# Token stage of an adaLN-attention-FFN kernel: the last VectorE operation of a weight unit stands behind the second normalising, GpSimd's scaling behind the token combination

## What is computed

```python
x = x + attn(einsum('bct,bcd->bdt', x, weights[conditions]))      # 16 heads, 8 kv heads, rope, top 25 of 64 keys by a router
h = x @ W.T + scaling[a] * (x @ A[a].T) @ B[a].T                  # a = adapter of the sequence
x = x + (gelu_tanh(h @ dequant(gate).T) * (h @ dequant(up).T)) @ dequant(down).T
```

## Time and profile before

| | us |
|---|---|
| median of 3 runs | 2812.93 |
| lowest, highest | 2810.95, 2813.51 |
| profiled execution | 2812.71 |
| its span, first to last instruction | 2811.1 |
| TensorE busy | 2669.4 (95%) |
| VectorE busy | 2182.8 (78%) |
| ScalarE busy | 1227.2 (44%) |
| GpSimd busy | 995.2 (35%) |

### The profile page before, as it was taken

The page is one execution under the profiler, slowest core; times in us unless marked ns, Lnnn a source line. Parts: engine busy times, 40 slices in busy tenths (PEclk is TensorE's granted clock), DMA queues, the critical chain, the costliest instruction groups (busy, mean ns, idle before and its releaser), DMA issues.

```text
span 2811.1 us, 54312 instructions
## 1 busy us (share of the span) xinstructions
PE 2669.4 (95%) x19200; PEld 2446.2 (87%) x19200; DVE 2182.8 (78%) x3724; ACT 1227.2 (44%) x2425; POOL 995.2 (35%) x1189
## 2 busy tenths in 40 slices
PE   5888998898899999999999999999999999999998
PEld 4777887787789999999999999999999999999998
DVE  6877777877578888888888888888888888756555
ACT  3445445454344444444444444444444444444443
POOL 4454434434244343434344343434334343300000
PEclk7999999999999999999999999999999999999999
DMA  3223232322676586668667766966776686657552
GB/s 119 74 97 100 78 98 87 102 75 94 237 283 246 215 341 252 256 237 346 228 231 294 309 228 223 358 259 226 268 314 248 233 311 264 235 213 282 190 193 88
DMA packets 197576, 599.87 MB, mean 213 GB/s; under 512 B 21224, under 2 KB 80488, under 8 KB 185200
## 3 DMA queue, kind: packets, MB, share of 16 engines
q1 hardware_dynamic: 162160, 496.89, 48.1%
q0 software_dynamic: 35328, 101.82, 9.7%
HBM read 417.83 MB, written 180.75 MB: 213 GB/s over the span
## 4 chain that ended last, share of the span: by engine, by line
PE 76%; DVE 15%; issue 4%; ACT 2%; DMA 2%; POOL 1%; SPq 0%; DVEq 0%; POOLq 0%; ACTq 0%
PE bank_a L881 22%; PE down L889 21%; PE bank_b L881 12%; PE proj L711 11%; PE bank_c L881 6%; DVE inter L1426 2%; DVE inter L1417 1%; DVE lut_line L1215 1%; PE scores L751 1%; PE scores L760 1%; DVE inter_parts L1433 1%; ACT inter L1128 1%; DVE hs L1242 1%; PE pv L776 1%; DVE probs L1308 1%
## 5 line engine op out<-in xcount | busy, mean ns | idle before, releaser
L881 PEld LDWEIGHTS bank_a<-h_in,gu_slot 128*128 128x128 f32 x6144 | 855.7, 190 | 74.0 <-ACT copy_p L1164 8.7
L881 PE MATMUL bank_a<-h_in,gu_slot 128*128 128x256 f32 x6144 | 899.0, 282 | 6.0 <-ACT copy_p L1164 5.8
L889 PE MATMUL down<-d_slot,inter_parts 128*128 128x512 f32 x3072 | 835.8, 394 | 2.0 <-DVE inter_parts L1433 2.0
L889 PEld LDWEIGHTS down<-d_slot,inter_parts 128*128 128x128 f32 x3072 | 527.6, 190 | 68.8 <-DVE inter_parts L1433 2.4
L881 PE MATMUL bank_b<-h_in,gu_slot 128*128 128x256 f32 x3072 | 456.3, 284 | 17.5 <-DVE up_val L1439 17.5
L592 POOL TENSOR_TENSOR lut_v<-lut_v,signed_scale 128x512 f32<-128x512 f32 x96 | 123.7, 1289 | 871.3 <-DVE lut_v L1231 871.0
L881 PEld LDWEIGHTS bank_b<-h_in,gu_slot 128*128 128x128 f32 x3072 | 404.5, 192 | 25.0 <-DVE up_val L1439 25.0
L1166 ACT ACTIVATE gate_val<-bank_a 128x256 f32<-128x256 f32 x256 | 98.1, 383 | 429.7 <-PE bank_a L881 429.7
L1413 DVE TENSOR_TENSOR up_val<-bank_b,copy_p 128x256 f32<-128x256 f32 x256 | 108.2, 423 | 205.6 <-PE bank_b L881 205.6
L1433 DVE TENSOR_TENSOR inter_parts<-inter,inter_parts 128x512 fp32r<-128x512 f32 x256 | 204.7, 800 | 33.3 <-ACT inter_parts L1132 33.3
L1426 DVE SCALAR_TENSOR_TENSOR inter<-inter,gate_val 128x512 f32<-128x512 f32 x256 | 204.8, 800 | 28.0 <-ACT inter L1128 27.7
(11 more groups left out here) (123 smaller groups left out, 3695.3 us busy)
## 6 DMA issues: line engine op xcount, KB each, us to landing
h_in<-h_scratch SPq DMA_DIRECT2D x64, 3584.0 KB, 13.1
acc<-out SPq DMA_DIRECT2D x64, 1024.0 KB, 5.4
out<-acc SPq DMA_DIRECT2D x64, 1024.0 KB, 4.3
gu_slot<-w_scratch SPq DMA_DIRECT2D x32, 1792.0 KB, 10.0
w_scratch<-w_parts POOLq DMA_DIRECT2D x96, 512.0 KB
h_scratch<-h_out SPq DMA_DIRECT2D x32, 896.0 KB, 5.0
d_scratch<-w_parts POOLq DMA_DIRECT2D x32, 512.0 KB
d_slot<-d_scratch SPq DMA_DIRECT2D x32, 512.0 KB, 15.4
```

The lines of the kernel that those rows point to most:

```text
L881: ins = pe.matmul(bank[:, 0:HALF], lhsT, rhs, start=(start and n == 0), stop=(n == len(pairs) - 1), skip_group_check=True)
L889: ins = pe.matmul(down[tc][:].rearrange("p (k h) -> p k h", k=2), inter_parts[:, j % 2, u, tc * P:(tc + 1) * P], d_slot[j][:, :, v, :], st ...
```

## The change

```diff
@@ GpSimd, iteration(t)
                     store_unit(*UNITS[t - 1][-1])
                 if t + MIXES < NT:
                     gather(t + MIXES)
-                scale_unit(*UNITS[t][0])
                 if t > 0:
                     spread(t, t - 1, 0)
+                scale_unit(*UNITS[t][0])
                 if t < NT - 1:
                     k_low(t + 1)
@@ VectorE, iteration(t)
                 softmax_shift(t, 1)
                 if do_head:
                     mixed(t + 1, (0, 1))
-                dequantise(*first, 4, DQ)
+                dequantise(*first, 4, DQ - 1)
                 if do_head:
                     mixed(t + 1, (2, 3))
                 softmax_sum(t, 1)
                 normalise(t, 1)
+                dequantise(*first, DQ - 1, DQ)
                 heads_low(t, 0)
```

## The result

| | before | after |
|---|---|---|
| median, us | 2812.70 (4 runs, 2810.95 to 2813.51) | 2795.14 (4 runs, 2790.40 to 2796.13) |
| profiled execution, us | 2812.71 | 2794.52 |
| its span, us | 2811.1 | 2793.0 |

The ratio is 0.9937, with a 95% interval of 0.9925 to 0.995: 17.6 us faster. The forecast was 2798.1, 14.6 us faster, with a range of 2792 to 2807.

What follows compares the result with a forecast made beforehand. In the token stage the chain runs over VectorE up to the routing and over TensorE behind it. From 2812.7 us, 9.8 for shorter waits and 4.8 for the clock leave 2798.1, range 2792 to 2807.

Steps and rivals of the forecast that it cites:

- Waits for `hs`: TensorE ahead of the routing, and in the last iteration: moving operation 7 off the path saves 9.8 us in sum.
- The clock: TensorE from routing to second turning: shorter waits mean three falls to 1.2 GHz fewer, 4.8 us.
- the two guesses behind the term: Falls of TensorE's clock expected after the change: two in nine regular iterations, three in five long ones.
- The cover: VectorE behind the normalising of half 1: operation 7 there, with its wait for GpSimd's store, delays nothing TensorE needs.
- The contention with GpSimd: VectorE instructions with both inputs in SBUF contend with GpSimd's SBUF reads; operation 7 and the rotation's multiplications are open to it.
- A: TensorE's clock falls as often as before, leaving only 9.8 us of gain: 2803 us; chance 0.20.
- B: Gain lost at the next wait, ScalarE's k placing and copies; some 3 us left: 2810 us; chance 0.14.
- C: GpSimd's scaling meets VectorE's k rotation at L1261: 9.3 us slower, 2822 us; chance 0.05.
- D: Nearly all falls of TensorE's clock go, 12.7 us besides the 9.8: 2790 us; chance 0.06.

Runs made afterwards that it cites:

- the repeat: The changed kernel run again without an edit, beside the filler runs on the same chip: 2796.41 us, ratio 0.9934.
- The filler runs: Matmuls with unused output added ahead of each token-stage routing: ten in the kernel before, 2802.96 us; seven in the changed kernel, 2791.61 us.
- VectorE's half alone: Changed kernel with GpSimd's old order, scaling ahead of `spread` of half 0; operation 7 stays behind the normalising: 2816.54 us, ratio 1.0015.
- with seven: Changed kernel with seven additional matmuls, output unused, ahead of each token-stage routing: 2791.61 us, ratio 0.9921.

## Why the prediction was right, and where it was off

**Waits for `hs`: right, in each part.** Nine iterations times 0.43 us was forecast, and 1.45 to 1.02 is 0.43. Iteration 2 gave 1.39 (1.35 forecast), iteration 8 gave 1.86 (1.84), 10 gave 0.74 and 14 gave 0.72 (0.71). The last iteration gave 0.5 (0.6). The sum was 9.8 and is 9.7 in the trace. The reason why it can be had so closely is that in each iteration the next limit was looked up: ScalarE's copies in nine, the end of operation 6 in five.

**The clock: right mechanism, term too small, and a loss left out.** The term was 4.8 us, three falls fewer of 1.6 us. The profile has 8.55 us, five falls fewer. The profile of the repeat has four falls and 65.31 us, so 7.0 us. Against it stand the 2.7 us at the low clock behind the last second turning, in both profiles, a place that the prediction doesn't look at. Net of them the clock gave 5.8 and 4.4 us, so it is partly luck that the term of 4.8 comes near: two errors stand against each other. What the medians leave is 17.6 - 9.7 = 7.9 us for the clock in all places, the start of the stage with its differences between executions included; where the 3 us beyond the forecast of 14.6 come from stays open. Of the two guesses behind the term, three falls in five long waits was right: the runs show 16 in 25. Two in nine for the waits of 1.0 us was wrong: they show 2 in 45. I had set them near the 3 in 9 of the waits of 1.45 us, but with 0.43 us less wait nearly all of them are gone. In iteration 2 a fall became cheaper as well: its stretch takes 5.67 us, against 6.81 in the earlier trace rows. The filler runs show by another way that it is the clock: they leave the order of VectorE alone, add work, and gain 9.7 us in the kernel before and 4.8 in the changed one.

**The cover: right.** Operation 7 behind the normalising costs nothing on VectorE: L1261 starts 5.9 us behind the routing, as before (337.38 against 331.47, 346.26 against 340.36 in the earlier trace rows). The margin of the scaling to it is 1.4 us as worked out, `k_low` still waits 2.33 us (2.3), the normalising takes 1.22 us (1.21), and the shift beside `spread` takes 1.23 us as in the earlier trace rows. The contention with GpSimd that the prediction set against the change cost next to nothing at the new places: operation 7 took 0.68 or 0.69 us in each iteration, and the k rotation's L1261 0.69 to 0.71, but in iteration 10, where it took 1.14 us (1.20 before the change).

**The rivals.** A (clock as before) would have left the fourteen stretches at 72.3 us. They are at 63.8. B (lost at the next wait) is refuted between the routing of iteration 1 and the last second turning, where the time is shorter by the whole sum of the terms. Its 2810 also didn't follow from what it named: the nine iterations are 3.9 of 9.8 us, and "a little" for the rest would have to be 2.9. But VectorE's half alone shows a form of B that the prediction hadn't named as one: with the old GpSimd order the gain goes to `spread` and ScalarE's split. The prediction saw `spread` and costed its move as harmless, and didn't say what it was for. C (the scaling meets the rotation) didn't come, for the reason given, its margin; placed behind the rotation, the scaling holds up `k_low`, and the kernel gets 21 us slower than the changed one. D (nearly all falls go) would be 2790. The fillers reach it, 2791.6 with seven; the change alone gets more than half way.

## What to carry to other kernels

Before an operation is moved off the path, look up what is queued behind its result on the other engines: here the move alone cost 4 us, and with the one reordering on GpSimd that it needs it gained 17.6. Value a shorter wait of TensorE by two terms, the wait itself and the clock behind it, and count falls by length of wait over all repeats of the pattern before guessing the second. When the terms add up to the difference of two spans, look whether they also do so part by part: here a gain and a loss that were no terms cancelled. Where such a wait can't be removed, a few matmuls without use in it may be worth more than they cost.

## What the runs showed of the hardware

The granted clock falls from 2.4 to 1.2 GHz behind waits of only 1.45 to 1.95 us, not in each execution and not in the same iterations: in 5 of 18 at 1.45 us and 16 of 25 at 1.7 to 1.95. A fall cost 1.3 to 1.6 us, and 2.5 in one iteration of the kernel before. With ten matmuls of 0.14 us each ahead of the routing, none of the kernel before's fourteen stretches behind it held a fall, where eight had. Up to the routing of iteration 1 the same program took 109.54 us in one execution and 113.94 in another.

Where a GpSimd operation ran beside a VectorE operation with two inputs in SBUF, one or both took longer: the scaling took 2.08 us instead of 1.29 beside an operation of 1.09 us, and an addition of `spread` took 0.90 instead of 0.45 beside the rotation's multiplication, which itself took 0.95 instead of 0.69. The Trainium skill, "SBUF — State Buffer", section "Who interferes with whom", says that the order of issue decides which of the two blocks. The trace agrees for the scaling, which started 0.17 us behind VectorE's operation (348.36 against 348.19) and ended 0.8 us late. In the earlier trace rows it doesn't: there the normalising started 0.41 us ahead of the scaling (253.07 against 253.48), and it was the normalising that took 2.83 us, while the scaling took its 1.29. So by the starts in these traces the order doesn't tell which of the two is held up. GpSimd's loads, 1.29 us for two, took the same time in all of these places.
